# A graph layer on one core: the turn from its first phase to its second, written as one list of steps

## The chip, the core and the metric

The kernel runs on one core of a Trainium2 chip. The core has five engines with a queue of instructions each: TensorE (PE; its weight loads are PEld), VectorE (DVE), ScalarE (ACT), GpSimd (POOL) and SyncE (SP, which only issues transfers here). Each runs its own queue in order and waits on semaphores that the others count up. Transfers run on 16 DMA engines. The metric is the device time of the program in microseconds (us), from runs without a profiler.

## What is computed

The input has 6250 nodes of 256 features and 100000 edges, sorted by their target node, with 16 kinds of edge. Cut to what matters:

```python
xn = layernorm(x)
msg = einsum('ni,rio->rno', xn, W)[rel_type, src] * norm            # 16 relations
gnn = segment_sum(msg, dst)
k = softmax(xn @ Wk, over all nodes);  context = k.T @ (xn @ Wv)    # per head
mix = ((xn @ Wq) @ context) * sigmoid(gelu(ln(xn) @ Wg1 + bg1) @ Wg2 + bg2) @ Wproj + bproj
x1 = x + gnn + mix
t = layernorm(x1)
out = x1 + t + sum over e of combine[:, e] * (gelu(t @ w1[e] + b1[e]) @ w2[e] + b2[e])   # 8 experts, the best 2 weigh
```

## The kernel before

The nodes are 49 tiles of 128 (the last has 106), and two tiles make a pair; there are 24 pairs and one tile more. All products on TensorE are float32 as two reduced parts, a high and a low one, so that a product is three passes; where a part is not split, TensorE takes a float32 product as two instructions.

**The first phase** goes over the 49 tiles. It makes the 16 relations' rows of each tile and stores them to a table in HBM (SP issues four pieces for each tile, line 523), stores the key and value rows of each tile (`kv_d`), and from tile 24 on it also sums the first three edge blocks of each row of eight, and folds the keys of the tiles 0 to 23 into a running context.

**The second phase** goes over the pairs. A pair has eight groups of edge blocks (three and two blocks by turns, 20 in all; group S = 8 i + s). For each group GpSimd gathers the rows from the table, one indirect transfer for each block (`gathers`, line 814), into a ring of four groups, so that the gathers of group S wait until the sums of group S - 4 are done; ScalarE scales the rows (`MSGS`), VectorE makes the 0/1 selection (`SELECT`), TensorE sums (`SUMS`), VectorE adds the sums to the nodes (`adds`). Beside the groups of pair i stand the mixer of pair i - 1 (`OUT`, `GATES`, `GATE`, `PROJ`, `STATS`, `MEAN`, `NORM`, `TURN`), and the eight experts of pair i - 2 (`LAYER1`, `LOW`, `LAYER2`, `ADD`); the table `SLOTS_OF_PAIR` gives this order for eight slots. `STATS` gives the variances, GpSimd makes roots of them between two gathers (`roots2`, lines 823 and 824), and only then can `MEAN`, `NORM`, `TURN` and the first `LAYER1` of the pair follow.

**Between the two** stands the turn that is changed. The keys of the 25 tiles that are not yet folded in have to be shifted by their maximum, raised with Exp and multiplied with the values: four tiles are held in SBUF (`held_shifts`, `held_exps`, `held_contexts`), 21 come back from `kv_d` in six parts of four and three rows by turns (SP line 569; `shifts` line 1536, `exps` line 992, `contexts` line 1977). Parts 0 and 1 land in `slot`, the space of the first phase's edge sums, the others in `later`. When the last row is in, a chain of five steps turns the context into the weights of the query (`finish_context`, `context_turn`, `context_values`, `head_contexts`, `query_context`, `query_high`, `query_low`); the first `OUT` needs them. The experts' weights come in four chunks of 1 MB through two buffers (`load_chunk`, line 560) and are split by ScalarE (line 843) and VectorE (line 1182). In this turn the pairs 0 and 1 use the gathered rows whole (`WHOLE = 2`): no high and low parts, TensorE takes two float32 instructions of 256 columns for a block in place of two of the reduced kind. For pair 0 the slots hold only groups and the context; for pair 1 they are those of `SLOTS_OF_SECOND`; from pair 2 on those of `SLOTS_OF_PAIR`. So the experts of pair 0 other than the first two stand beside the groups of pair 2.

The order of the work on an engine is thus written out by hand, by slots: each engine runs, slot by slot, what the table names for it, with the work of the turn ahead of or behind the slot.

## Time and profile before

| what | value |
|---|---|
| time, three runs | 1601.41, 1601.22, 1599.69 us; median 1601.22 |
| span of the profiled execution | 1685.8 us, 84.6 us over the median |
| TensorE busy in it | 1601.8 us, 95% |
| VectorE, GpSimd, ScalarE busy | 79%, 59%, 57% |
| first phase | to about 779.7 us |
| turn, with the pairs 0 to 2 | about 779.7 to 891.4 us |
| each pair after that | about 34.0 us |

The profiled execution is one run with the profiler on; its own time is given only by its span, and it is longer than the runs without. Times of single instructions and distances between them are read from it; the median of the runs is what a change is counted against.
### The profile page before, as it was taken

What the parts mean: (1) busy time and instruction counts of PE and PEld (TensorE: products, weight loads), DVE (VectorE), ACT (ScalarE), POOL (GpSimd) and SP (SyncE); (2) the same over time, 40 slices, a digit from 0 to 9 for tenths busy, and PEclk for the clock granted to TensorE, in tenths of its full rate; (3) what the DMA queues carried; (4) which work ended last, traced back from release to release, by engine and by line L of the source; (5) the groups of instructions that cost most, each with busy time, mean ns of one, the idle gap of its engine ahead of it and who ended that gap; (6) DMA issues with size and microseconds to landing.
All of it is one profiled execution on the core that took longest, in us unless ns stands there. A gap on an engine that the chain in (4) does not pass through costs nothing.

```text
span 1685.8 us, 31748 instructions
## 1 busy us (share of the span) xinstructions
PE 1601.8 (95%) x10509; PEld 1451.7 (86%) x10509; DVE 1340.2 (79%) x3389; ACT 961.4 (57%) x2156; POOL 999.6 (59%) x1111
## 2 busy tenths in 40 slices
PE   7999999999999989998789999999999999999998
PEld 6888888777877878786689999999999999999998
DVE  7888565577777777775569999889999999999985
ACT  4444322345555555554566767667766777666764
POOL 4533322766676666673766767666766666666630
PEclk9999999999999999998999999999999999999999
DMA  9776656677877877787633333333333333333320
GB/s 295 267 258 246 235 226 238 222 242 242 259 249 242 257 228 252 238 265 271 203 98 100 108 104 112 100 102 101 117 101 106 101 116 100 99 109 110 104 62 10
DMA packets 127076, 290.50 MB, mean 172 GB/s; under 512 B 21271, under 2 KB 49724, under 8 KB 126914
## 3 DMA queue, kind: packets, MB, share of 16 engines
q1 hardware_dynamic: 86068, 177.19, 28.9%
q0 software_dynamic: 39952, 110.13, 24.1%
...
## 4 chain that ended last, share of the span: by engine, by line
PE 67%; DVE 12%; issue 8%; ACT 6%; another core or an unknown queue 3%; POOL 2%; DMA 1%; SPq 0%; DVEq 0%; ACTq 0%; POOLq 0%
PE bank L1821 52%; PE bank L2025 3%; PE bank L2026 2%; PE bank L1865 2%; PE bank L1866 2%; ACT mh L1030 2%; DVE ml L1606 2%; DVE ml_a L1357 1%; POOL stg L814 1%; PE bank L1977 1%; DVE ht L1722 1%; DVE xres L1736 1%; ACT raw L1086 1%; DVE stg L1224 1%
## 5 line engine op out<-in xcount | busy, mean ns | idle before, releaser
L814 POOL DMA_INDIRECT stg<-table,idxcur x495 | 530.6, 1072 | 263.9 <-issue 172.9
L1821 PE MATMUL bank<-wreg,xt 128*128 128x512 f32 x2352 | 589.9, 401 | 7.3 <-issue 6.5
L1821 PEld LDWEIGHTS bank<-wreg,xt 128*128 128x128 f32 x2352 | 438.6, 191 | 100.5 <-issue 11.4
L696 POOL DMA_INDIRECT raw<-table,idxa x297 | 302.5, 1018 | 147.3 <-issue 85.4
L1821 PE MATMUL bank<-tt,wreg 128*128 128x256 f32 (+1 forms) x2400 | 319.5, 282 | 0.0
L1821 PE MATMUL bank<-wreg,ht 128*128 128x256 f32 x2352 | 314.7, 283 | 0.4 <-DVE ht L1722 0.2
L1821 PEld LDWEIGHTS bank<-tt,wreg 128*128 128x128 f32 x2400 | 296.4, 189 | 2.9
L1821 PEld LDWEIGHTS bank<-wreg,ht 128*128 128x128 f32 x2352 | 293.2, 189 | 0.9 <-DVE ht L1722 0.4
L1086 ACT ACTIVATE raw<-bank,cols 128x256 f32<-128x256 f32 (+1 forms) x400 | 164.4, 462 | 132.7 <-remote 72.6
L1224 DVE COPY stg<-bank 128x512 f32<-128x512 f32 x196 | 134.2, 686 | 110.4 <-PE bank L1821 76.1
L1606 DVE SCALAR_TENSOR_TENSOR ml<-stg,nrm,mh 128x256 fp32r<-128x256 f32 x455 | 195.5, 478 | 13.4 <-ACT mh L1030 12.8
L860 ACT COPY stg<-bank 128x512 f32<-128x512 f32 x196 | 112.8, 582 | 156.3 <-PE bank L1821 124.8
L1030 ACT ACTIVATE mh<-stg,nrm 128x256 fp32r<-128x256 f32 x455 | 200.9, 499 | 0.0
L1736 DVE SCALAR_TENSOR_TENSOR xres<-bank,raw,xres 128x256 f32<-128x256 f32 x392 | 169.8, 473 | 21.6 <-PE bank L1821 11.7
L885 ACT ACTIVATE mh_a<-raw,nrm 128x256 fp32r<-128x256 f32 x297 | 128.9, 502 | 73.6 <-DMA raw<-table,idxa 49.6
L1091 ACT CAST ht<-raw 128x512 fp32r<-128x512 f32 (+1 forms) x200 | 122.5, 613 | 59.6 <-PE bank L1821 49.3
L1357 DVE SCALAR_TENSOR_TENSOR ml_a<-raw,nrm,mh_a 128x256 fp32r<-128x256 f32 x297 | 126.0, 477 | 37.1 <-issue 28.2
L1722 DVE TENSOR_TENSOR ht<-raw,ht 128x512 fp32r<-128x512 f32 (+1 forms) x200 | 134.9, 675 | 22.7 <-ACT ht L1091 20.6
L2025 PE MATMUL bank<-mh,sel 128*128 128x256 f32 x455 | 126.5, 304 | 4.1 <-DVE ml L1606 3.0
L2026 PE MATMUL bank<-ml,sel 128*128 128x256 f32 x455 | 118.4, 281 | 0.0
L1590 DVE TENSOR_TENSOR sel<-dbl,dpr 128x384 fp32r<-128x384 f32 x198 | 95.0, 480 | 9.8 <-PE bank L2021 7.7
L1865 PE MATMUL bank<-mh_a,sel_a 128*128 128x256 f32 x297 | 86.0, 314 | 13.3 <-DVE ml_a L1357 7.8
...
## 6 DMA issues: line engine op xcount, KB each, us to landing
...
```

The lines of the kernel that those rows point to most:

```text
L696: pool.indirect_dma_start(ring_a[:, r * EARLY + j, :], None, table[0:LIMIT, :], bass.IndirectOffsetOnAxis(ap=idxa[:, at:at + 1], axis=0)). ...
L814: pool.indirect_dma_start(stg[:, (s % 4) * SUP + j, :], None, table, bass.IndirectOffsetOnAxis(ap=idxcur[:, at:at + 1], axis=0)).then_inc( ...
L1030: act.activation(mh[:, (s % 2) * CUT + j, :], stg[:, (s % 4) * SUP + j, :], ACT.Copy, scale=nrm[:, bass.ds(at + j, 1)]).then_inc(msg_hi, 1)
L1086: act.activation(hf[e % 2][:, c * 256:c * 256 + nt * P], bank[2 + e % 2][:, c * 256:c * 256 + nt * P], ACT.Gelu, bias=b1c[:, 2 * e + c:2 * ...
L1224: dve.tensor_copy(stage[:, j // 2, (j % 2) * 512:(j % 2 + 1) * 512], bank[3 + j % 4][:]).then_inc(copied(k, j)[0], 1)
L1357: dve.scalar_tensor_tensor(out=ml_a[:, m + j, :], in0=ring_a[:, r * EARLY + j, :], scalar=nrm[:, bass.ds(EB * q + j, 1)], in1=halves(mh_a[ ...
L1606: dve.scalar_tensor_tensor(out=ml[:, m, :], in0=stg[:, (s % 4) * SUP + j, :], scalar=nrm[:, bass.ds(at + j, 1)], in1=halves(mh[:, m, :]), ...
L1722: dve.tensor_tensor(ht[e % 2][:, LO, :, 0:n], cols2(hf[e % 2], n), halves(ht[e % 2][:, HI, :, 0:n]), ALU.subtract).then_inc(h_lo, 1)
L1736: dve.scalar_tensor_tensor(out=xk, in0=bank[6 + e % 2][:, a * C:(a + 1) * C], scalar=comb[:, a, e:e + 1], in1=xk, op0=ALU.mult, op1=ALU.ad ...
L1821: mm = pe.matmul(dst, stat(a, c), mov(b, c), start=(n == 0), stop=(n == 3 * chunks - 1))
L2025: pe.matmul(bank[u % 2][:, 0:C], sel[:, m, :], mh[:, m, :], start=(s % 2 == 0 and j == 0), stop=False)
L2026: mm = pe.matmul(bank[u % 2][:, 0:C], sel[:, m, :], ml[:, m, :], start=False, stop=(s % 2 == 1 and j == PART[1] - 1))
```

## The change

- The slots of the pairs 0, 1 and 2 go. One list, `CHANGE`, holds all steps of the turn and of these pairs, and every engine runs in the list's order those steps that it has a part in (`follow`). From pair 3 on `SLOTS_OF_PAIR` is used as before.
- Five of the seven rows of `slot` are asked back by SP within the last tile of the first phase, behind its second table piece (`FREE_ROWS`); the other two follow the last of the kept contexts. VectorE's shifts and ScalarE's Exp of the parts 0 and 1 stand ahead of the wait for the end of the first phase.
- A weight chunk is split in two halves on each engine (`SPLIT n h`), and the splits stand elsewhere in the order.
- The first `LAYER1` of pair 0 stands ahead of the sums of group 11 (before: behind those of group 12), and experts of pair 0 stand among the last sums of pair 1. For this the experts' scratch (`hf`, `comb` and others) leaves the buffer of the weight chunks for space of its own (`cd`, `mix`, `wv`).
- Four groups more, 20 in all, use whole rows (`WHOLE_GROUPS`).
- The roots of pair 0 stand ahead of the second gather of group 12 (before: ahead of the first of group 13). The Gelu table is loaded early by a step of its own.

```diff
-    ROOTS, FIRST_ROOTS = (7, 1), (5, 0)
+    ROOTS, EARLIER_ROOTS = (7, 1), {1: (4, 1), 2: (5, 0)}
+    FREE_ROWS = 5
-        hf = [rs[:, 2048 + 512 * b:2560 + 512 * b] for b in range(2)]
+        ctxbd = cd[:, 0:C].rearrange("p (c n) -> p c n", c=CC)
+        dg = cd[:, C:2 * C]
+        hf = [cd[:], wv[:].rearrange("p c n -> p (c n)")]
...
@@ SP, stores of a tile @@
+                    if at(k, NT - 1) and h == 1:
+                        sp.wait_ge(sum_a, ER)
+                        for b2 in range(2):
+                            sp.wait_ge(kv_st[b2], 16 * ((KEPT + SLOTS) // 2))
+                        for n in range(FREE_ROWS):
+                            load_row(n // 4, n)
...
+            def load_row(part, n):
+                sp.dma_start(rows_of(part)[:, n, :], kv_d[group(group_of(part))[n]]).then_inc(kv_in[part], 16)
...
-            load_rows(0)
-            load_rows(1)
+            sp.wait_ge(ctx1_mm, KEPT)
+            for n in range(FREE_ROWS, SLOTS):
+                load_row(1, n)
             first_phase_over(sp)
...
             for n in range(4, 6):
-                sp.wait_ge(w_lo, n + 1)
+                sp.wait_ge(w_lo, splits_of(n, 1))
                 load_chunk(n + 2)
@@ ACT @@
+            def SPLIT(n, h):
+                act.wait_ge(raw_in[n % 2], 32 * (n // 2 - 1))
+                if n >= 6:
                     act.wait_ge(ctx_mm, HELD + REST)
+                act.copy(wreg[:, HI, place_of(n), h * CC // 2].rearrange("p r o -> p (r o)"),
+                         raw[:, n % 2, h * WC * C:(h + 1) * WC * C]).then_inc(w_hi, 1)
+            def GELU_TABLE():
+                act.activation(small[0:1, 156:157], small[0:1, 157:158], ACT.Gelu).then_inc(table_kept, 1)
             held_exps()
+            for ready in range(2):
+                EXP(ready)
             first_phase_over(act)
@@ DVE @@
+            for ready in range(2):
+                SHIFT(ready)
             dve.wait_ge(flag_ready, 1)
...
-PARTS_OF_SLOT = {0: (0, 1), 1: (2,), 2: (3,), 3: (4,), 4: (5,)}
-SPLITS = ((0, 4), (0, 5), (1, 0), (1, 1))
-SPLITS_LOW = ((0, 5), (0, 6), (1, 1), (1, 3))
-WHOLE = 2
+WHOLE_GROUPS = 20
...
+CHANGE = (
+    "HELD_ROWS", "ROWS_OF 0", "FADE", "SELECT 0 0", "SELECT 0 1", "SHIFT 2", "EXP 2", "ROWS_OF 1", "MSGS 0 0", "SUMS 0 0",
+    "ROWS_OF 2", "SHIFT 3", "EXP 3", "MSGS 0 1", "SUMS 0 1", "SELECT 0 2", "ROWS_OF 3", "SHIFT 4", "EXP 4",
+    "MSGS 0 2", "SUMS 0 2", "SHIFT 5", "EXP 5", "ADDS 0 0", "SELECT 0 3", "MSGS 0 3", "SUMS 0 3", "ROWS_OF 4",
+    "SELECT 0 4", "ADDS 0 1", "GELU_TABLE", "MSGS 0 4", "SPLIT 4 0", "SPLIT 4 1", "SELECT 0 5", "ROWS_OF 5",
+    "CONTEXT", "SUMS 0 4", "CONTEXT_PE", "MSGS 0 5", "CONTEXT_TURN", "SUMS 0 5", "VALUES", "SELECT 0 6", "HEADS",
+    "QUERY", "MSGS 0 6", "CLEAR", "ADDS 0 2", "QUERY_ROWS", "GATES 0 2", "GATE_ACT 0 2", "SUMS 0 6", "OUT 0 2",
+    "SELECT 0 7", "MSGS 0 7", "SPLIT 5 0", "SUMS 0 7", "SELECT 1 0", "GATE 0 2", "GATE_HI 0 2", "MSGS 1 0", "SUMS 1 0",
+    "ADDS 0 3", "GATE_LOW 0 2", "PROJ 0 2", "SELECT 1 1", "SPLIT 5 1", "MSGS 1 1", "SUMS 1 1", "ADDS 1 0", "STATS 0 2",
+    "SELECT 1 2", "MSGS 1 2", "SUMS 1 2", "SPLIT 6 0", "MEAN 0 2", "NORM 0 2", "SPLIT 6 1", "TURN 0 2", "TURN_HI 0 2",
+    "TURN_LOW 0 2", "MSGS 1 3", "SELECT 1 3", "LAYER1 0 2 0", "LOGIT 0 2", "SUMS 1 3", "LAYER1 0 2 1", "TOP 0 2",
+    "LOW 0 2 0", "ADDS 1 1",
+    "WEIGHT 0 2", "SELECT 1 4", "LOW 0 2 1", "SPLIT 7 0", "COMB 0 2", "COMB_HI 0 2", "MSGS 1 4", "LAYER1 0 2 2",
+    "LAYER2 0 2 0", "OUT 1 2", "SUMS 1 4", "GATES 1 2",
...
+    "ADD 0 2 6", "LAYER1 1 2 0", "LOGIT 1 2", "MSGS 2 5", "LAYER2 0 2 7", "LOW 1 2 0", "SUMS 2 5", "LAYER1 1 2 1", "TOP 1 2",
+    "ADD 0 2 7", "ADDS 2 2", "SELECT 2 6", "MSGS 2 6", "SUMS 2 6", "SELECT 2 7", "MSGS 2 7", "SUMS 2 7",
 )
...
+def follow(order, **steps):
+    for entry in order:
+        name, *numbers = entry.split()
+        if name in steps:
+            steps[name](*map(int, numbers), *((8,) if name in OF_GROUPS else ()))
...
-    for s in range(8):
-        slot_of(0, s, 8, None, 0, None, 0)
-    for s in range(8):
-        slot_of(1, s, 8, 0, 2, None, 0)
-    for i in range(2, pairs):
+    for i in range(3, pairs):
```

In the part of the list that is left out, the other steps of the experts of pair 0 (`LAYER1`, `LOW`, `LAYER2`, `ADD`) stand one by one among the groups 13 to 21, with the mixer of pair 1; `SPLIT 7 1` stands behind the sums of group 13.

## Rows read from the trace of the kernel before

**Rows 1.** Windows by stage: length, busy time and instructions by engine, clock, DMA share.

```profile
779.70:812.90 33.20, 28.75 (x122) 24.48 (x121) 13.34 (x22) 15.40 (x26) 21.73 (x25) 0.90 0.99 336
812.90:842.60 29.70, 19.44 (x98) 15.05 (x98) 19.91 (x38) 16.58 (x30) 22.69 (x20) 0.90 0.54 163
842.60:857.50 14.90, 10.62 (x50) 9.35 (x48) 4.71 (x16) 7.82 (x18) 9.43 (x11) 0.73 0.31 86
857.50:891.40 33.90, 33.36 (x278) 32.69 (x277) 28.73 (x77) 22.21 (x52) 22.92 (x26) 1.00 0.34 100
891.40:925.40 34.00, 33.18 (x278) 32.65 (x277) 31.09 (x88) 23.20 (x55) 23.83 (x24) 1.00 0.33 102
```

**Rows 2.** The chain of waits: start, us, what (tile, line, count).

```profile
798.61 3.47 PE bank L1977 x16
802.07 1.29 PE bank L2021 x6
...
891.46 4.20 PE bank L1821 x36
...
925.50 4.20 PE bank L1821 x36
```

**Rows 3.** Timeline of TensorE in the turn: start, us, instruction, [idle before <- releaser].

```profile
779.73 3.63 PE L1968 MATMUL bank<-kvs 128*128 128x257 f32 x16
787.80 8.64 PE L1977 MATMUL bank<-slot 128*128 128x257 f32 x28 [4.45 <-ACT slot L992]
...
806.67 6.23 PE L1977 MATMUL bank<-later 128*128 128x257 f32 x28
...
842.63 2.26 PE L1821 MATMUL bank<-tt,wreg 128*128 128x256 f32 x12
```

**Rows 4.** Timeline of SyncE's transfers, from the last tile on: start and us of issuing.

```profile
769.29 6.10 SPq L523 DMA_DIRECT2D table<-stg  x3
...
778.16 0.32 SPq L523 DMA_DIRECT2D table<-stg  x1
778.59 3.80 SPq L569 DMA_DIRECT2D slot<-kv_d  x7
782.84 7.04 SPq L569 DMA_DIRECT2D later<-kv_d  x14
```

**Rows 5.** Windows of 5 us, columns as in the first group.

```profile
770.00:775.00 5.00, 5.00 (x27) 4.19 (x26) 2.81 (x6) 2.92 (x6) 0.00 (x0) 1.00 0.53 211
...
785.00:790.00 5.00, 2.20 (x5) 1.83 (x6) 3.63 (x7) 1.91 (x2) 4.08 (x4) 0.57 1.02 348
```

**Rows 6.** Timeline of VectorE in the turn.

```profile
781.02 0.42 DVE L1379 TENSOR_TENSOR raw<-raw,bank 128x257 f32<-128x257 f32 x1 [0.47 <-DVE raw L1379]
785.43 1.23 DVE L1536 TENSOR_TENSOR slot<-slot,dg 128x1024 f32<-128x1024 f32 x1 [3.99 <-DMA slot<-kv_d]
...
817.64 2.27 DVE L1182 TENSOR_TENSOR wreg<-raw,wreg 128x2048 fp32r<-128x2048 f32 x1
...
833.59 0.25 DVE L1661 BATCH_NORM_AGGREGATE small<-small 128x2 f32<-128x6 f32 x2
...
839.80 0.68 DVE L1672 TENSOR_TENSOR tt<-bank,tt 128x512 fp32r<-128x512 f32 x1
```

**Rows 7.** Timeline of ScalarE: Exp of part 0, and the first gathered rows.

```profile
786.69 1.06 ACT L992 ACTIVATE slot<-slot 128x1024 f32<-128x1024 f32 x1 [6.09 <-DVE slot L1536]
...
791.50 1.31 ACT L1026 ACTIVATE stg<-stg,nrm 128x256 f32<-128x256 f32 x3 [2.21 <-DMA stg<-table,idxcur]
```

**Rows 8.** Timeline of GpSimd: gathers 1, 11, 21 and 43 of the second phase.

```profile
782.28 0.99 POOL L814 DMA_INDIRECT stg<-table,idxcur  x1 [1.27 <-DMA table<-stg]
...
798.53 0.94 POOL L814 DMA_INDIRECT stg<-table,idxcur  x1 [3.01 <-issue]
...
814.97 0.94 POOL L814 DMA_INDIRECT stg<-table,idxcur  x1 [3.85 <-issue]
...
849.05 0.95 POOL L814 DMA_INDIRECT stg<-table,idxcur  x1 [0.30 <-issue]
```

More of the change, by code:

```diff
@@ L804, in gathers @@
                     for j in range(PART[s % 2]):
-                        if (s, j) == (FIRST_ROOTS if isinstance(i, int) and i == 1 else ROOTS) and not (isinstance(i, int) and i < 1):
+                        if (s, j) == EARLIER_ROOTS.get(i, ROOTS) and not (isinstance(i, int) and i < 1):
                             roots2(i - 1, 2)
@@ L1022, in MSGS @@
                 at = EB * (4 * i + s // 2) + EARLY + (s % 2) * CUT
-                if isinstance(i, int) and i < WHOLE:
+                if whole(S):
                     for j in range(n):
@@ L1527, in _, with SHIFT @@
             keep_contexts(NT - 1, NP, 1, 0)
-            dve.wait_ge(flag_ready, 1)
-            far = dve.value_load(flag[0:1, 0:1], min_val=0, max_val=NT * P * R)
-            first_phase_over(dve)
-            def shifts(part):
+            def SHIFT(part):
                 a, b = span_of(part)
@@ L1766, in slot_of @@
             def slot_of(i, s, groups, p1, n1, p2, n2):
-                if isinstance(i, int) and i + s == 0:
-                    for part in PARTS_OF_SLOT[0]:
-                        shifts(part)
-                    fade_kept()
                 in_slot(i, s, groups, p1, n1, p2, n2, SELECT=SELECT, MSGS=MSGS, WINDOW=WINDOW, LAST_WINDOW=LAST_WINDOW, GATE=GATE,
@@ L1773, in slot_of @@
                         BIAS2_ADD=BIAS2_ADD, LOW=LOW, ADD=ADD)
-                if isinstance(i, int):
-                    if i == 0 and s > 0:
-                        for part in PARTS_OF_SLOT.get(s, ()):
-                            shifts(part)
-                    if (i, s) in SPLITS_LOW:
-                        split_lo(4 + SPLITS_LOW.index((i, s)))
-                if isinstance(i, int) and (i, s) == (0, 5):
-                    finish_context()
-                if isinstance(i, int) and (i, s) == (0, 6):
-                    head_contexts()
-                    dve.memset(halves(c3[:]), 0.0).then_inc(c3_clear, 1)
-                if isinstance(i, int) and (i, s) == (0, 7):
-                    query_low()
+            follow(CHANGE, SHIFT=SHIFT, FADE=FADE, SPLIT=SPLIT_LOW, CONTEXT=CONTEXT, CONTEXT_TURN=CONTEXT_TURN, HEADS=HEADS,
+                   CLEAR=CLEAR, QUERY_ROWS=QUERY_ROWS, SELECT=SELECT, MSGS=MSGS, ADDS=ADDS, GATE=GATE, GATE_LOW=GATE_LOW,
+                   STATS=STATS, MEAN=MEAN, TURN_LOW=TURN_LOW, TOP=TOP, COMB=COMB, COMB_LOW=COMB_LOW,
+                   BIAS2_ADD=BIAS2_ADD, LOW=LOW, ADD=ADD)
             run(slot_of, NP, TAIL_GROUPS)
@@ L1953, in _ @@
             pe.wait_ge(k_shift_diag, 2)
-            pe.matmul(bank[1][:, C:2 * C], halves(ones[:]), dg[:], start=True, stop=True).then_inc(kmb_mm, 1)
+            pe.matmul(bank[1][:, C:2 * C], halves(ones[:]), dg, start=True, stop=True).then_inc(kmb_mm, 1)
             pe.wait_ge(flag_ready, 1)
@@ L2151, in _ @@
             pe.wait_ge(add_a, ALL_ADDS)
+            follow(CHANGE, HELD_ROWS=HELD_ROWS, ROWS_OF=ROWS_OF, CONTEXT_PE=CONTEXT_PE, VALUES=VALUES, QUERY=QUERY,
+                   SUMS=SUMS, OUT=OUT, GATES=GATES, PROJ=PROJ, TURN=TURN, LOGIT=LOGIT, COMBT=COMBT, BIAS2=BIAS2,
+                   LAYER1=LAYER1, LAYER2=LAYER2)
             run(slot_of, NP, TAIL_GROUPS)
@@ L2181 @@
 )
[L2184 to L2193 removed]
+OF_GROUPS = ("SELECT", "MSGS", "SUMS", "ADDS")
+CHANGE = (
[4 rows of a table added]
+    "CONTEXT", "SUMS 0 4", "CONTEXT_PE", "MSGS 0 5", "CONTEXT_TURN", "SUMS 0 5", "VALUES", "SELECT 0 6", "HEADS",
[22 rows of a table added]
+)
+def follow(order, **steps):
[3 more added lines that the diff above has]
+            steps[name](*map(int, numbers), *((8,) if name in OF_GROUPS else ()))
 def in_slot(i, s, groups, p1, n1, p2, n2, **steps):
[L2199 removed]
+    for entry in SLOTS_OF_PAIR[s]:
         name, *expert = entry[1:].split()
```

156 lines of the change are left out of this document (62 added, 94 removed), and 12 rows, old and new, of the table CHANGE.

## The prediction, made before the changed kernel had run

> **What bounds the kernel now.** I read the stages first, then the chain of waits across the turn, then the timeline of each engine in it. The profiled execution spans 1685.8 us, 84.6 us more than the median of the runs (1601.2 us). I work out microseconds in the profiled execution and take the same number off the median; I have no row that says where the profiler's 84.6 us lie.
>
> From pair 3 on a pair takes 34.0 us, and TensorE is busy for 33.2 us of it at full clock [rows 1, 2]: the second phase is TensorE's. So the change can only move the instant at which this even pace begins: in the chain it begins with the 36 matmuls at 891.46 (`LAYER1 2` and `LAYER2 0` of pair 1, `OUT` of pair 2), and the next pair at 925.50 [rows 2]. I call 891.46 the hand-over. All work ahead of it is the same before and after, apart from four groups that become whole.
>
> The turn starts with the held rows at 779.73 [rows 3]; 111.7 us to the hand-over. In the first two stages TensorE is busy 28.75 of 33.2 and 19.44 of 29.7 us, in the third 10.62 of 14.9 at a mean clock of 0.73 [rows 1]. So some 19 us are idle, and part of the rest runs at half clock. The whole gain that is to be had lies there.
>
> **Part 1, key rows earlier.** Before, SP issues seven rows behind the last table piece, at 778.59 to 782.39 [rows 4]. VectorE is free at 781.44 and then waits 3.99 us for part 0; TensorE stands idle 4.45 us, and its next 28 matmuls take 8.64 us [rows 3, 6]. At full pace 16 such take 3.47 us [rows 2], so 28 take 6.07: 2.6 us went to the clock, whose mean is 0.57 in that window [rows 5]. After, five rows are issued behind table piece 1, that is between the first and the last of the three pieces issued from 769.29 to 775.39 [rows 4], by my reading at about 772 to 775. The DMA engines are 0.53 busy there [rows 5], so these rows should be in by 780. `SHIFT 0` can then start at 781.4, is 1.23 us, Exp 1.06 us [rows 6, 7], so TensorE goes on at about 783.8, against the held rows' end at 783.4. Idle and slow clock save 4.0 + 2.6 = 6.6 us at this place.
>
> Some is given back. The list puts `SUMS 0 0` ahead of part 2, and the scaling of the first gathered rows waits for their transfers until 791.50 + 1.31 [rows 7]. The first gather's own start, 782.28, waits for the last table piece (778.16) [rows 4, 8], and this isn't moved. So TensorE, through with part 1 at about 790, waits until about 792.3 for `SUMS 0 0`. What remains from there: the groups 0 to 3, 10 blocks of 0.43 (three take 1.29 [rows 2]) = 4.3, and 14 rows of 0.434 (two chunks of two instructions, 3.47 / 16 each, is 0.87 a row) = 12.1 us: 808.7. Before, the last row ended at 806.67 + 6.23 = 812.9 [rows 3]. **Term 1: -4.2 us.** Bounds: 0 (the DMA engines, 0.99 busy through this stage [rows 1], bring the later rows no sooner) and -6.6.
>
> **Part 2, from the last row to the first expert.** Before, the variances of pair 0 end at 833.84 (833.59 + 0.25), 20.9 us behind the last row. On that path VectorE's step on the heads stood behind a whole weight split of 2.27 us (817.64) [rows 6]. In the list `SPLIT 4` stands ahead of `CONTEXT`, while VectorE waits for the rows, and `SPLIT 5 0` behind `OUT`: 2.2 us go. **Term 2: -2.2.** Bounds 0 (another wait of VectorE, for `MSGS` or sums, in its place) and -4.9: gathers 21 on begin when `SUMS 0 4` is through, 814.97 now [rows 8]; by the list at 810.1, if the rows end at 808.7 and the three blocks follow.
>
> Then the first `LAYER1`. Before, 833.84 to 842.63 is 8.8 us [rows 3, 6]: `TURN_LOW` ended at 840.48, then three blocks of sums went first, 2.15 us. In the list these stand behind. GpSimd now waits for the variances with its roots (before it was busy with a gather, about 1.6 us), but one half of `SPLIT 6` comes between, about 1.2 us on VectorE and nearly as much on ScalarE; I let these cancel. **Term 3: -2.2**, bounds 0 and -3.8. The first `LAYER1` then starts at 842.6 - 8.6 = 834.0. The roots wait behind `STATS`: gather 32 and all behind it stand still until then, some 3 us by my times, counted with the gathers below.
>
> **Part 3, from the first expert to the hand-over.** Price list [rows 2]: a reduced matmul of 256 columns is 4.20 / 36 = 0.117 us; an expert's layer is 12 of them, 1.40. TensorE still has after `LAYER1 0`'s start: 18 layers (10 `LAYER1`, 8 `LAYER2`) 25.2; `OUT` and `PROJ` 2.8; the groups 11 to 19 whole, 22 blocks of 0.43, 9.5; groups 20 to 23, 10 blocks of two matmuls, 2.3; gates, turns, logits twice and biases, some 28 small ones (in a pair's 278 instructions [rows 1] 22 are such), 3.3. Sum 43.1 us. Before, the same stretch had 7 whole and 20 reduced blocks, so 25.2 + 2.8 + 3.0 + 4.7 + 3.3 = 39.0, and took 891.46 - 842.63 = 48.8 [rows 2, 3]: 9.8 us lost, nearly all ahead of 857.5.
>
> The four groups that become whole cost TensorE 10 x 0.2 = 2.0 us (in the 43.1) and save VectorE work that isn't on the path: it has 4.71 + 28.73 us in that stretch [rows 1], less than 37 even with two chunks' splits on top. After, there is expert work for TensorE wherever it waited for sums. I take the loss of an even pair (34.0 less 32.5 of work = 1.5; here 2.0) and one stretch of slow clock as after the idle of part 1 (2.6): 4.6 us. 834.0 + 43.1 + 4.6 = 881.7. **Term 4: 47.7 for 48.8, -1.1 us.** Bounds: a loss of 2.0 (-3.7) and of 9.8 (+4.1).
>
> At no cost: the merged buffers; SP's five issues (table pieces 2 and 3 become ready at about 775 and 778, behind them); the table load, which ends ahead of `MSGS 0 4` while the rows are on their way (uncovered it is one ACT step of about the size of an Exp); chunk 7, asked for when `SPLIT 5 1` is subtracted (about 823) and first needed behind 838.
>
> **Sum.** -4.2 - 2.2 - 2.2 - 1.1 = -9.7: hand-over at 881.7, span 1676, median 1601.2 - 9.7 = **1591.5 us**.
>
> **Rivals.**
>
> *The gathers set the pace.* 43 gathers took 782.28 to 850.0 [rows 8]; less the two stalls (3.01, 3.85) 1.42 us each, copies and roots in it. The first 60 then take 85 us, to 867.3; sums follow some 6 us later: 873, 8 us ahead of TensorE. But if both stalls stay (6.9) and the roots add 3, it is 883, and with one stall more 886: the gain is then 5 to 8 us, **1595**. For it: each of the 13 groups still needs its gathers. Against: the list lets TensorE clear the ring sooner.
>
> *The earlier rows bring nothing.* The stage is 0.99 full of transfers [rows 1], and if the table's last pieces, and with them the first gathers, get later for the five rows (5 x 128 x 513 x 4 bytes = 1.31 MB, 3.9 us at this stage's 336 GB/s), term 1 is lost and most of term 2, which leaves 2 to 4 us, **1599**. For it: nothing but transfers bounds 784 to 792. Against: 0.53 before that [rows 5], and piece 3 is only issued at 778.16 [rows 4], some 3 us behind the last of the five rows. I give it 0.13. The Trainium skill, "DMA: Bandwidth & Descriptors", section "Queues, rings and completion order", says that on each DMA engine the descriptors of SP's queue are consumed in ring order. By that rule the five rows go ahead of the pieces 2 and 3 and this rival comes out; no row of this trace shows two such transfers in each other's way.
>
> *Slower: the clock stays down.* From 842.6 to 857.5 TensorE ran at 0.73 though it had work for most of the time [rows 1]. In the list it has to wait for the roots at about 826 to 833, and then meets sums whose gathers may not be in, two groups between experts towards the end. If half of the 43.1 us (21.5 at full pace) runs at 1.2 in place of 2.4 GHz, that costs 21.5 us in place of my 2.6, and the time is 1591.5 + 19 = 1610; the gain is gone from about 10 us of such work beyond mine, and I put the case at **1606**. Against: experts are 1.4 us each and wait for nothing that is gathered. The Trainium skill, "TensorE: Matmul & The Clock Gate", Part 1, says that the throttled clock is the default and activity releases it; the drop behind the idle 4.45 us agrees with it.
>
> **How the numbers follow.** My forecast, 4 to 15 us gained (1586 to 1597), 0.57; gathers 0.15; rows bring nothing 0.13; slower 0.12; more than 15 us, 0.03. Within 0.2% (3.2 us) a measurement of this kernel can't be told from no change; nearly all of the third case lies there. Faster 0.76, same 0.12, slower 0.12. The range leaves out the gain over 16 us, which the gathers hardly allow (873), and most of the slower case: 1585 to 1602.
>
> **What would show it.** Right: rows end near 809, first expert near 834, the pair-3 matmuls near 882, and pairs of 34.0 behind; shifts of part 0 without a wait on a transfer; the clock full from about 838. Wrong: `SUMS 0 0` later than 794 (term 1); GpSimd's gather 21 still near 815 (term 2); TensorE idle or at half clock among the experts (term 4); a second pace in which gathers come back to back up to the hand-over.

## The result: slower, and the profile after

The changed kernel takes 1621.6 us (median of 4 runs, 1619.9 to 1623.9) against 1601.3 us for the kernel before on the same chip: a ratio of 1.0122 (95% interval 1.0104 to 1.0140), 20.3 us slower. 1591.5 was forecast, with 1602 as the upper end.

The rows of before that stand above come from an execution of 1685.8 us. In a second one, of 1600.0 us, the turn itself was 6.3 us shorter (the held rows' start to the hand-over: 105.4 for 111.7). I compare with that one from here on. These are its windows by stage: held rows to last key row, on to the first `LAYER1`, on to the hand-over, one pair. The columns are those of [rows 1].

```profile
721.70:753.80 32.10, 28.15 (x122) 24.04 (x121) 13.00 (x22) 14.56 (x25) 21.31 (x25) 0.95 1.03 346
753.80:783.50 29.70, 19.43 (x99) 14.99 (x97) 20.36 (x38) 17.54 (x30) 22.65 (x20) 0.89 0.54 165
783.50:827.20 43.70, 40.28 (x325) 39.30 (x324) 33.42 (x94) 29.91 (x67) 32.95 (x34) 0.99 0.36 104
827.20:860.40 33.20, 33.20 (x278) 32.72 (x277) 31.35 (x88) 23.73 (x56) 24.56 (x26) 1.00 0.37 108
```

The same four stages of the changed kernel:

```profile
718.90:751.00 32.10, 28.30 (x122) 23.93 (x121) 13.27 (x20) 16.14 (x28) 22.59 (x26) 0.95 0.95 316
751.00:779.20 28.20, 17.19 (x89) 13.66 (x88) 16.09 (x35) 13.83 (x27) 17.58 (x19) 0.84 0.55 170
779.20:845.30 66.10, 51.55 (x333) 47.84 (x334) 35.28 (x97) 34.16 (x77) 31.55 (x37) 0.91 0.26 76
845.30:878.40 33.10, 33.10 (x269) 32.96 (x269) 28.76 (x75) 21.50 (x49) 23.22 (x25) 0.95 0.35 101
```

The first stage is as long as before, the second 1.5 us shorter, the pair behind the hand-over as long. The third, from the first `LAYER1` to the hand-over, is 22.4 us longer. TensorE is busy for 51.55 of its 66.1 us. The prediction put its work there at 43.1 us; so 14.55 us are idle, and 8.4 us are busy time beyond that work. Before, it was 40.28 of 43.7 us for 39.0 us of work: 3.4 idle, 1.3 beyond.

Most of the 8.4 us is the slow clock, not all. These are the windows of the changed kernel's third stage whose granted clock lies furthest below 1:

```profile
779.20:784.00 4.80, 4.80 (x21) 4.74 (x22) 0.47 (x3) 1.46 (x3) 2.97 (x4) 0.50 0.36 96
784.00:789.00 5.00, 5.00 (x29) 4.71 (x28) 2.13 (x10) 1.20 (x3) 2.14 (x3) 0.68 0.14 44
832.00:838.00 6.00, 5.94 (x38) 5.73 (x38) 2.06 (x6) 2.27 (x5) 4.41 (x6) 0.75 0.33 101
```

Busy time times what the clock lacks of 1 gives 2.4, 1.6 and 1.5 us; the rest of the stage adds 0.2. That is an estimate of 5.6 us for the clock. The other 2.8 us aren't explained; a part may be that a row ahead of a wait counts to the end of its last matmul: the twelve at 796.63, ahead of a wait, take 1.58 us, while 1.39 us behind the start of the twelve at 795.24 the next row begins. Before, the mean clock of the stage was 0.99, so at most 0.4 of the 1.3 us is clock.

TensorE's timeline of before in its second execution, from the held rows to the hand-over:

```profile
721.71 3.63 PE L1968 MATMUL bank<-kvs 128*128 128x257 f32 x16
...
747.53 6.23 PE L1977 MATMUL bank<-later 128*128 128x257 f32 x28
...
783.47 1.99 PE L1821 MATMUL bank<-tt,wreg 128*128 128x256 f32 x12
...
827.11 1.57 PE L1821 MATMUL bank<-tt,wreg 128*128 128x256 f32 x12
```

And in the changed kernel:

```profile
718.88 3.63 PE L1979 MATMUL bank<-kvs 128*128 128x257 f32 x16
722.35 3.63 PE L1988 MATMUL bank<-slot 128*128 128x257 f32 x16
726.32 2.87 PE L1988 MATMUL bank<-slot 128*128 128x257 f32 x12 [0.34 <-ACT slot L1004]
732.65 2.90 PE L2032 MATMUL bank<-stg,sel 128*128 128x256 f32 x6 [3.47 <-ACT stg L1040]
...
744.75 6.23 PE L1988 MATMUL bank<-later 128*128 128x257 f32 x28
...
779.17 2.93 PE L1832 MATMUL bank<-tt,wreg 128*128 128x256 f32 x12 [2.66 <-DVE tt L1691]
...
800.00 1.10 PE L2032 MATMUL bank<-stg,sel 128*128 128x256 f32 x4 [1.78 <-ACT stg L1040]
...
805.19 1.53 PE L2032 MATMUL bank<-stg,sel 128*128 128x256 f32 x6 [1.26 <-ACT stg L1040]
...
831.89 0.55 PE L2036 MATMUL bank<-mh,sel 128*128 128x256 f32 x1 [2.73 <-DVE ml L1622]
...
843.05 0.36 PE L2036 MATMUL bank<-mh,sel 128*128 128x256 f32 x1 [2.60 <-DVE ml L1622]
...
845.23 2.76 PE L1832 MATMUL bank<-tt,wreg 128*128 128x256 f32 x12
```

The last row is the hand-over. Behind the first `LAYER1` each group of sums waits for its messages. The brackets of this stage add up to its idle 14.5 us: 7.1 us for ScalarE's messages (1.78, 1.26, 1.27, 1.27, 1.26 and 0.30), 5.9 us for the low parts of the last groups (2.73, 0.29, 2.60, 0.32), 1.46 us for a selection. ScalarE's timeline in one of these blocks says why the messages are late:

```profile
802.54 0.84 ACT L1100 ACTIVATE cd<-bank,cols 128x256 f32<-128x256 f32 x2 [1.35 <-PE bank L1832]
804.01 0.62 ACT L1105 CAST ht<-cd 128x512 fp32r<-128x512 f32 x1 [0.63 <-PE bank L1832]
804.54 1.30 ACT L1040 ACTIVATE stg<-stg,nrm 128x256 f32<-128x256 f32 x3
```

The messages (line 1040) wait for no transfer: they stand in the list behind `LAYER1`'s copy, and the copy waits for TensorE's `LAYER2` of two experts earlier. TensorE then does `SUMS` and waits for the messages; the next expert waits behind the sums. GpSimd meanwhile waits for TensorE, not TensorE for it:

```profile
807.51 0.94 POOL L830 DMA_INDIRECT stg<-table,idxcur  x1 [2.99 <-PE bank L2032]
```

So in this block TensorE and ScalarE take turns: the first layers at 795.24, 800.75 and 806.70 are 5.5 and 6.0 us apart, where the even pace has eight slots in 33.2 us, 4.2 each.

### The profile page after: what moved, and what is told of

It reads as the page before. It is cut to its first block, busy times and chain, and to the rows that moved or that the text cites. A ratio compares the mean times of both kernels' runs of the same rounds, so it can differ in the third digit from the quotient of the medians.

```text
span 1618.1 us, 31745 instructions
## 1 busy us (share of the span) xinstructions
PE 1571.3 (97%) x10509; PEld 1441.1 (89%) x10509; DVE 1338.5 (83%) x3383; ACT 966.3 (60%) x2161; POOL 1010.4 (62%) x1111
## 3 DMA queue, kind: packets, MB, share of 16 engines
q8 instruction: 85, 1.39, 0.4%
## 4 chain that ended last, share of the span: by engine, by line
PE 90%; DVE 3%; issue 2%; ACT 2%; DMA 1%; POOL 1%; SPq 0%; ACTq 0%; DVEq 0%; POOLq 0%
PE bank L1832 71%; PE bank L2036 4%; PE bank L2037 3%; PE bank L1876 2%; PE bank L1877 2%; PE bank L2032 1%; PE bank L1887 1%; PE bank L1988 1%; PE bank L2076 1%; PE bank L2088 1%; DMA xres<-in_L_gnn_weight 1%; PE bank L1842 1%; DVE pad L1262 1%; PE bank L2085 1%; DMA stg<-table,idxcur 0%
## 5 line engine op out<-in xcount | busy, mean ns | idle before, releaser
L830 POOL DMA_INDIRECT stg<-table,idxcur x495 | 543.1, 1097 | 238.5 <-issue 149.1
L1832 PE MATMUL bank<-wreg,xt 128*128 128x512 f32 x2352 | 578.1, 396 | 0.9 <-DVE wreg L1189 0.4
L1832 PEld LDWEIGHTS bank<-wreg,xt 128*128 128x128 f32 x2352 | 432.9, 188 | 88.8 <-ACT stg L872 1.2
L1622 DVE SCALAR_TENSOR_TENSOR ml<-stg,nrm,mh 128x256 fp32r<-128x256 f32 x445 | 190.9, 477 | 15.3 <-ACT mh L1044 15.2
L1044 ACT ACTIVATE mh<-stg,nrm 128x256 fp32r<-128x256 f32 x445 | 196.4, 499 | 0.3 <-PE bank L2037 0.3
L1755 DVE SCALAR_TENSOR_TENSOR xres<-bank,mix,xres 128x256 f32<-128x256 f32 x392 | 169.4, 472 | 18.2 <-PE bank L1832 17.5
L1100 ACT ACTIVATE wv<-bank,cols 128x256 f32<-128x256 f32 (+1 forms) x200 | 82.5, 464 | 68.4 <-PE bank L1832 68.4
L1100 ACT ACTIVATE cd<-bank,cols 128x256 f32<-128x256 f32 (+1 forms) x200 | 82.5, 463 | 46.3 <-PE bank L1832 46.3
L677 POOL TENSOR_TENSOR xres<-xres,bpb 128x256 f32<-128x256 f32 x24 | 20.7, 863 | 131.4 <-DVE kvs L1224 131.3
L2036 PEld LDWEIGHTS bank<-mh,sel 128*128 128x128 f32 x445 | 84.2, 189 | 11.5 <-issue 6.2
```

The source lines that it names most:

```text
L830: pool.indirect_dma_start(stg[:, (s % 4) * SUP + j, :], None, table, bass.IndirectOffsetOnAxis(ap=idxcur[:, at:at + 1], axis=0)).then_inc( ...
L1044: act.activation(mh[:, (s % 2) * CUT + j, :], stg[:, (s % 4) * SUP + j, :], ACT.Copy, scale=nrm[:, bass.ds(at + j, 1)]).then_inc(msg_hi, 1)
L1100: act.activation(hf[e % 2][:, c * 256:c * 256 + nt * P], bank[2 + e % 2][:, c * 256:c * 256 + nt * P], ACT.Gelu, bias=b1c[:, 2 * e + c:2 * ...
L1622: dve.scalar_tensor_tensor(out=ml[:, m, :], in0=stg[:, (s % 4) * SUP + j, :], scalar=nrm[:, bass.ds(at + j, 1)], in1=halves(mh[:, m, :]), ...
L1755: dve.scalar_tensor_tensor(out=xk, in0=bank[6 + e % 2][:, a * C:(a + 1) * C], scalar=comb[:, a, e:e + 1], in1=xk, op0=ALU.mult, op1=ALU.ad ...
L1832: mm = pe.matmul(dst, stat(a, c), mov(b, c), start=(n == 0), stop=(n == 3 * chunks - 1))
```

## The experiments

For each kernel the table gives three instants, in us from the start of its held rows in its profiled execution (the first phase ends at 718.9 to 725.0, differently in each execution, so spans alone don't compare), the stretch from the first `LAYER1` to the hand-over, and the timed runs. The kernel before has 32.1, 61.8, 105.4 and 43.6; the changed one 32.1, 60.3, 126.4 and 66.1. The runs come from several chips, so times are compared by the ratios, each against the kernel before on the same chip.

| Kernel | rows end | first LAYER1 | hand-over | stretch | median us | ratio to before (95%) |
|---|---|---|---|---|---|---|
| e1, before again | 32.1 | 61.8 | 105.4 | 43.6 | 1601.7 (one run) | |
| e2, messages ahead | 32.9 | 61.1 | 119.5 | 58.4 | 1613.9 | 1.0063 (1.0043 to 1.0084) |
| e4, 16 whole groups | 32.5 | 60.6 | 129.5 | 68.9 | 1627.0 | 1.0146 (1.0122 to 1.0170) |
| e3b, rows late | 34.1 | 60.6 | 126.8 | 66.2 | 1622.9 | 1.0120 (1.0103 to 1.0137) |
| e5, e2 + split 6 late | 33.6 | 60.0 | 118.2 | 58.2 | 1613.0 | 1.0054 (1.0034 to 1.0074) |
| e6, e5 + rows 2 first | 32.7 | 61.0 | 117.3 | 56.3 | 1608.8 | 1.0034 (1.0021 to 1.0047) |
| e7, experts in the old pace | 32.1 | 60.3 | 113.0 | 52.7 | 1608.5 | 1.0033 (1.0021 to 1.0046) |
| e13, old second half | 32.9 | 62.0 | 107.7 | 45.7 | 1601.2 | 0.9999 (0.9988 to 1.0009) |
| e8, a list for each engine | 26.3 | 54.7 | 115.2 | 60.6 | 1611.2 | 1.0051 (1.0033 to 1.0069) |
| e9, e8 with rows late | 31.7 | 61.4 | 117.7 | 56.3 | 1612.2 | 1.0055 (1.0037 to 1.0072) |
| e10, two sums to an expert | 25.4 | 55.2 | 121.1 | 65.9 | 1616.0 | 1.0073 (1.0056 to 1.0090) |
| e11, e8 + old pace | 26.3 | 56.1 | 109.6 | 53.4 | 1602.6 | 0.9995 (0.9985 to 1.0005) |
| e12, e11 mended | 25.8 | 54.8 | 104.6 | 49.8 | 1599.1 | 0.9979 (0.9964 to 0.9995) |

**e1, the kernel before once more, for a second profile.** No edit. It gave the windows above.

> The kernel before, unchanged, once more with a profile, since its first profiled execution was 84.6 us longer than its runs while that of the changed kernel (1618.1 us) agrees with its runs. If the surplus lay in the first phase (TensorE idle there), the held rows start at about 719 us as in the changed kernel, and turn plus pairs behind it make up the difference of 20 us: hand-over about 107 to 112 us behind the held rows, against 126.4 in the changed kernel. If the change also costs time in the first phase, the held rows start some 5 us earlier than 719.

**e2, the messages ahead on ScalarE.** The list of the changed kernel, with `MSGS` of groups 1 4 to 2 6 moved ahead of the `LAYER1` beside them:

```diff
-    "ADDS 1 2", "LAYER1 0 2 4", "LAYER2 0 2 2", "MSGS 1 6",
+    "ADDS 1 2", "MSGS 1 6", "LAYER1 0 2 4", "LAYER2 0 2 2",
```

> Only the order is changed: in the blocks with experts of pair 0 the scaling of the gathered rows (MSGS of groups 12 to 22) goes ahead of the expert's first layer in the list, as in the slots used before. Theory A (ScalarE's order): behind the first layer, ScalarE's copy of the hidden rows waits for TensorE's second layer, the scaling waits behind the copy and TensorE's sums wait for the scaling, which costs 1.3 to 2.7 us in each block, 14.6 us in the eleven gaps of the trace: about 1605 to 1609 us. Rival B (the gathers are late): the scaling would wait for its transfers in the new place too, no gain, 1619 to 1622. Rival C (whole rows load TensorE): no gain here either.

The idle time of the stretch fell from 14.5 to 7.7 us (2.22, 0.72, 2.31 and 2.47), the hand-over came 6.9 us sooner, the time fell by 8 to 9 us. TensorE's busy time hardly fell (50.67 us, at a mean clock of 0.88 for 0.91), so the slow clock didn't go with these waits. ScalarE's order is a third of the loss; it isn't all.

**e4, fewer whole groups.**

```diff
-WHOLE_GROUPS = 20
+WHOLE_GROUPS = 16
```

> The changed kernel with 16 whole groups in place of 20: groups 16 to 19 take a high and a low part. Rival C: 10 blocks cost TensorE 0.2 us less each, 2 us gained, 1619 to 1620. Theory A: VectorE's low parts come into the serial loop of each block as well, each group later by 0.9 to 1.3 us: 2 to 6 us slower, 1624 to 1628.

Not faster: the hand-over comes 3.1 us later, and the time is 3.8 us longer by the ratios, whose intervals overlap. So the larger load of TensorE isn't the cause of the loss. That the four whole groups help where sums stand among experts is likely, but not shown.

**e3b, the five early rows issued behind the last table piece again.**

```diff
-                    if at(k, NT - 1) and h == 1:
-                        sp.wait_ge(sum_a, ER)
...
-                        for n in range(FREE_ROWS):
-                            load_row(n // 4, n)
```

> The changed kernel with one thing undone: its first five key rows come back as late as in the kernel before, behind the last table piece. The list of steps stays. Theory A (the early rows brought nothing at the rows' end: in the changed kernel's trace the rows end 32.1 us after the held rows' start, as in the kernel before, 32.05): 1621.6 within 2.5 us, and the rows end at +32 to +34. Rival (the early rows are worth what was forecast): 3 to 5 us slower than the changed kernel, some 1626. Rival (the early rows delay the table's last pieces and the first gather, which starts at +4.07 for +2.64 before): 1 to 2 us faster, some 1620, with the first gather at +2.6.

The median is 1.3 us above the changed kernel's and the ratio the same; the rows end 2.0 us later, the first `LAYER1` comes 0.3 and the hand-over 0.5 us later. In this list the early rows bring nothing that lasts. Their price shows too. First SyncE and GpSimd of the changed kernel:

```profile
710.35 3.91 SPq L554 DMA_DIRECT2D slot<-kv_d  x5
714.36 0.38 SPq L539 DMA_DIRECT2D table<-stg  x1
715.59 0.32 SPq L551 DMA_DIRECT2D hg_d<-hgt  x1
...
721.01 0.31 POOL L757 MEMSET cd<- 128x256 f32 x1 [21.39 <-DMA hg_d<-hgt]
...
722.95 0.99 POOL L830 DMA_INDIRECT stg<-table,idxcur  x1 [0.29 <-POOL idxcur L752]
```

And of e3b:

```profile
719.29 0.32 SPq L545 DMA_DIRECT2D hg_d<-hgt  x1
...
721.22 0.31 POOL L756 MEMSET cd<- 128x256 f32 x1 [14.46 <-DMA hg_d<-hgt]
...
724.43 0.99 POOL L829 DMA_INDIRECT stg<-table,idxcur  x1 [1.37 <-DMA table<-stg]
```

GpSimd, which waits for `hg_d`, goes on 5.4 us after its issue behind five rows, and 1.9 us without them. The first gather starts 4.1 us behind the held rows' start for 2.7. The Trainium skill, "DMA: Bandwidth & Descriptors", section "Queues, rings and completion order", has the descriptors of SyncE's queue consumed in ring order; the 5.4 for 1.9 us agree with it. But the 16 DMA engines were busy for 0.98 of those 5.4 us (715.59 to 721.01) and for 0.25 of the 1.9 us (719.29 to 721.22), so engines full of rows account for the delay as well; no run separates the two.

**e5 and e6, the halves of split 6, and the third part of the rows.** Each on top of the one before:

```diff
-    "SUMS 1 2", "SPLIT 6 0", "MEAN 0 2", "NORM 0 2", "SPLIT 6 1", "TURN 0 2",
+    "SUMS 1 2", "MEAN 0 2", "NORM 0 2", "TURN 0 2",
...
-    "TURN_LOW 0 2", "MSGS 1 3", "SELECT 1 3", "LAYER1 0 2 0",
+    "TURN_LOW 0 2", "MSGS 1 3", "SELECT 1 3", "SPLIT 6 0", "SPLIT 6 1", "LAYER1 0 2 0",
...
-    "ROWS_OF 1", "MSGS 0 0", "SUMS 0 0", "ROWS_OF 2",
+    "ROWS_OF 1", "MSGS 0 0", "ROWS_OF 2", "SUMS 0 0",
```

> As e2 (messages ahead of the first layer's copy on ScalarE, 1613.9), and both halves of the split of weight chunk 6 moved from before and behind the normalisation to just ahead of the first expert's first layer. Theory A (the halves lie on the path from the roots to the first LAYER1, 2.2 us of it, and the engine's clock is down behind that wait): the first LAYER1 starts at +58 to +59 for +61.1 in e2, and the time is 1610 to 1612. Rival (the roots on GpSimd and the rest of the chain end last anyway): within 1.5 us of e2, the first LAYER1 at +60.5 or later.

> As e5, and the third part of the key rows goes ahead of the first sums in TensorE's order (the changed kernel let TensorE wait 3.47 us for the first message there, while the third part's exponential had been done 2.3 us before). Theory A (that order cost the rows' end): the rows end at +29 to +30 for +32 to +33, and the time is 2 to 3 us below e5. Rival (the rows' end is set by the landing of the later parts, or what follows waits for something else): the rows end within 1 us of e5's, and the time is within 1.5 us of e5's.

The first `LAYER1` comes 1.1 us sooner with e5, and that is lost again in e6's run. The times differ by 0.9 and 4.2 us, the hand-overs by 1.3 and 0.9 only, with overlapping intervals. With e5 the way from the variances to the first `LAYER1` takes 5.7 us for 7.4, so the halves did lie on the path, as its theory had it; but the time stayed within 1.5 us of e2, as the rival had it. The rows end with e6 within 1 us of e5, as its rival had it: putting part 2 first exchanged the wait for messages for one of 2.20 us for part 2's Exp, at half clock (5.42 us for 16 matmuls). Whether e6 gains time isn't told: its time fell by more than the rival's 1.5 us, its hand-over by 0.9.

**e7, the experts in the old pace.** Up to `TURN_LOW` the changed list with its roots, then `LAYER1 0 2 0`, the sums of groups 1 3 to 1 7 with `LAYER1 0 2 1` among them, and from `WEIGHT` on `SLOTS_OF_PAIR` written out for pair 2's groups, one to a slot (pair 2's groups in two products, as in the kernel before):

```diff
+    "MSGS 1 3", "SELECT 1 3", "LAYER1 0 2 0", "LOGIT 0 2", "SUMS 1 3",
...
+    "SUMS 1 5", "SELECT 1 6", "MSGS 1 6", "ADDS 1 2", "LAYER1 0 2 1", "SUMS 1 6", "SPLIT 7 0", "SPLIT 7 1",
+    "SELECT 1 7", "MSGS 1 7", "SUMS 1 7", "WEIGHT 0 2", "SELECT 2 0", "LOW 0 2 1", "MSGS 2 0",
...
```

> The changed kernel's list up to the first LAYER1 of pair 0, then the old order: the rest of pair 1's sums in a row beside the first two first layers, and the experts 2 to 7 with pair 2's groups in the even pace's own order. Theory A (the loss is in the list from the first LAYER1 on: 66.1 us for 43.1 us of work): that stretch takes 44 to 48 us as in the kernel before (43.8), and the time is 1600 to 1605. Rival B (gathers late, since GpSimd's first gather starts 1.4 us later and the roots are issued earlier): the stretch stays above 55 us, and the time above 1611. Rival C (the two-product sums moved to whole groups, or the split chunks, load the engine): the stretch stays above 55 us with TensorE's busy share above 0.95.

13.4 us of the hand-over are regained, not 21. Idle is 4.4 us here, but TensorE is busy for 48.31 of 52.7 us at a mean clock of 0.86: the first `LAYER1` still takes 2.93 us. It lies between the theory and its rivals: part of the loss must come from what e7 kept, the first `LAYER1` ahead of the sums and the early roots, or from the first half. It also has 16 whole groups again, as have e11, e12 and e13.

**e13, the new first half with the old second half.** As e7, but sums 1 3 and 1 4 ahead of the first `LAYER1`, and the roots at their old place:

```diff
+    "SELECT 1 3", "MSGS 1 3", "SPLIT 6 0", "MEAN 0 2", "NORM 0 2", "SPLIT 6 1", "SUMS 1 3", "SELECT 1 4", "ADDS 1 1",
+    "TURN 0 2", "TURN_HI 0 2", "MSGS 1 4", "TURN_LOW 0 2", "SUMS 1 4", "SELECT 1 5", "LAYER1 0 2 0", "LOGIT 0 2",
...
-    ROOTS, EARLIER_ROOTS = (7, 1), {1: (4, 1), 2: (5, 0)}
+    ROOTS, EARLIER_ROOTS = (7, 1), {1: (5, 0)}
```

> The changed kernel's list as far as the sums of group 1 2 (its early key rows, its order of rows and chain, its halves of the splits), and behind that the old kernel's order: sums of groups 1 3 and 1 4 ahead of the first LAYER1, the other three between it and the second, experts 2 to 7 in the old pace with pair 2's groups in two products, the roots at the old places. Theory (the whole loss comes from moving pair 1's sums behind the first LAYER1 and among the experts, and the first half is worth about nothing): pair 3's pace at +104 to +109 for +105.4 in the kernel before and +126.4 in the changed one, and 1600 to 1605 us. Rival (the first half also costs, by the later first gather and the split halves on the path): pace at +111 or later, 1607 or more. Other rival (the first half gains what was forecast, 8.6 us, once the second half does not hide it): pace at +101 or sooner, 1597 or less.

It takes as long as the kernel before. So the early rows, the order of rows and chain and the halved splits are together worth nothing that can be measured, and the whole loss lies in what the change does from group 1 3 on (experts, roots, whole groups). TensorE's timeline of e13 around the first `LAYER1`:

```profile
773.42 4.61 PE L2032 MATMUL bank<-stg,sel 128*128 128x256 f32 x10 [3.54 <-issue]
777.82 1.06 PE L2076 MATMUL bank<-ident,scr 128*128 128x128 f32 x4
780.05 1.53 PE L2032 MATMUL bank<-stg,sel 128*128 128x256 f32 x6 [1.17 <-DVE xres L1636]
781.24 1.75 PE L1832 MATMUL bank<-tt,wreg 128*128 128x256 f32 x12
```

The ten matmuls of groups 1 2 and 1 3 run at half clock (4.61 us; at full clock ten take 2.32) while the normalisation is worked out on other engines. The 3.54 us of idle time ahead of them stand in the changed kernel too: the sums of 1 2 start 0.6 us behind their selection in both kernels (773.42 behind 772.79, and 772.31 behind 771.68), which stands behind `STATS` on VectorE. The first `LAYER1` comes 1.7 us later than in the changed kernel, but takes 1.75 us for 2.93. In the changed kernel 1 3 is behind it. There the clock is already down when `TURN` comes (its four matmuls at 775.39 take 1.12 us for 0.60), TensorE then stands still for 2.66 us, and the experts pay for the slow clock: in the windows from 779.20 on, shown with the result, TensorE is busy throughout, at a granted clock of 0.50 (1.2 for 2.4 GHz) and then 0.68.

**e8 and e9, a list for each engine.** `CHANGE` becomes a list per engine; all rows go first, the sums into the waits of the chain. On VectorE:

```diff
-    "SELECT 0 0", "SELECT 0 1", "SHIFT 2", "SHIFT 3", "SELECT 0 2", "SHIFT 4", "SHIFT 5", "ADDS 0 0",
+    "SELECT 0 0", "SELECT 0 1", "SHIFT 2", "SHIFT 3", "SHIFT 4", "SHIFT 5", "SELECT 0 2", "ADDS 0 0",
```

> The steps of the changed kernel in a list of its own for each engine: all key rows ahead of the sums on VectorE, ScalarE and TensorE (the shifts of the last parts no longer behind a selection that waits for the first sums), the sums then in the waits of the chain from the context to the first LAYER1, halves of the weight splits in VectorE's waits, only six of pair 1's and pair 2's groups fewer behind the first LAYER1 than in the changed kernel, and messages ahead of the first layer's copy on ScalarE. Theory (each wait of the changed turn is one of order, and the gathers leave room): rows end at +26 to +28 for +32.1, first LAYER1 at +50 to +54 for +60.3, pair 3's pace at +95 to +102 for +126.4 (kernel before: +105.4), and 1590 to 1600 us. Rival (the gathers, which start at +4 to +6 with the early rows, set the pace through the sums that the chain needs): the first LAYER1 at +56 or later and 1603 or more.

> As e8, with the first five key rows as late as in the kernel before (behind the last table piece). Theory (the early rows hold up the landing of the last node's gate rows, which GpSimd waits for, and with it the first gather; with the sums in the chain's waits an earlier gather is worth more than earlier rows): first gather at +2.7 for +4 to +6, rows end at +28 to +30, first LAYER1 1 to 3 us sooner than in e8, and 1 to 3 us below e8. Rival (the rows set the chain's start and the gathers have room): 2 to 4 us above e8.

Here the rows do end sooner, at 26.3, and the first `LAYER1` comes at 54.7. What held the rows is to be seen on VectorE, first in e6, then in e8:

```profile
742.82 0.56 DVE L1605 TENSOR_TENSOR sel<-dbl,dpr 128x384 fp32r<-128x384 f32 x1 [4.61 <-PE bank L2032]
743.30 2.09 DVE L1545 TENSOR_TENSOR later<-later,cd 128x1024 f32<-128x1024 f32 x2
```

```profile
738.33 1.23 DVE L1545 TENSOR_TENSOR later<-later,cd 128x1024 f32<-128x1024 f32 x1 [2.80 <-DMA later<-kv_d]
741.49 0.96 DVE L1545 TENSOR_TENSOR later<-later,cd 128x768 f32<-128x768 f32 x1 [1.94 <-DMA later<-kv_d]
```

In e6 `SELECT 0 2` (the first row) waits 4.61 us for sums, and the shifts of parts 4 and 5 behind it then wait for no transfer: their rows were there. In e8 the shifts wait for the rows alone. With that gone the early rows are worth 5.4 us at the rows' end and 6.7 at the first `LAYER1` (e9 against e8), but 1.0 us of the time. The theory of e9, that the early rows cost more through the later gather than they bring, fell at these instants; the times can't tell the two apart. And all of the gain of e8 is gone at the hand-over: the stretch takes 60.6 us, and pace and time are far off what I expected.

**e10, e11 and e12, what stands behind the first LAYER1.** All from e8's first half; e10 has two groups to an expert, e11 has groups 1 4 to 1 6 ahead of the old pace and 1 7 in its first slot, e12 mends four places of e11, one of them on GpSimd:

```diff
-    ROOTS, EARLIER_ROOTS = (7, 1), {1: (4, 0)}
+    ROOTS, EARLIER_ROOTS = (7, 1), {1: (4, 0), 2: (6, 1)}
```

> As e8 up to the first LAYER1 (which e8 had at +54.7, 5.6 us sooner than the changed kernel), and behind it the same steps in another order: the experts' layers start at once, the sums that are left come two to an expert up to expert 6, so that pair 2's first two groups, which pair 1's statistics wait for, are summed by expert 5 and not by experts 5 and 6 with the turn behind the last expert. Theory (in e8 and in the changed kernel the pair's last chain, from the statistics through roots, normalisation and turn to the next pair's first LAYER1, lies bare behind expert 7, since its sums come too late: 816 to 836 in e8): no wait over 1 us there, pair 3's pace at +100 to +107 for +115.2 in e8, and 1595 to 1603 us. Rival (VectorE and ScalarE can't do two groups to an expert beside the layers): blocks of 6 to 7 us, pace at +112 or later, and 1608 or more.

> As e8 up to the first LAYER1, then pair 1's last groups ahead of the experts 2 to 7, and these in the old kernel's even pace with pair 2's groups one to a slot (the roots of pair 1 at the old place, all pair 2 groups in two products). Theory (the lists of rows and chain are worth some 7 us against the old kernel, and the experts in the old pace give none of it back): pair 3's pace at +100 to +104, 1595 to 1600 us, faster than the old kernel (1602.8) by 3 to 7. Rival (the gathers of pair 1's last groups, landing at +61 to +68, then set the start of the pace): pace starts at +72 or later, and 1602 to 1608.

> As e11, with four places mended that its trace names: pair 1's roots on GpSimd go ahead of five gathers (e11 had the statistics at 811.9 and the roots at 815.8, behind the gathers), the first LAYER1 goes ahead of the sums of group 1 3 on TensorE (e11's waited 1.3 us for these messages), the messages of group 1 4 ahead of the second first layer's copy on ScalarE (2.1 us), and the combination weights ahead of the third first layer's copy. Theory (the pair's chain behind the statistics costs the pace in e11 40.5 us for 32.9 in the kernel before): pace starts at +66 to +67 for +69.0, pair 3's pace at +100 to +104 for +109.6 in e11 and +105.4 in the kernel before, and 1594 to 1599 us. Rival (VectorE's and ScalarE's load in the pace with both halves of the last split and two-product sums, not the roots, made it slow): pair 3's pace at +107 or later, 1600 to 1603.

e10 is the slowest of the three: its theory fell. GpSimd waits 6.72 us with pair 1's roots, the gathers behind them come late, and the messages of group 2 4 wait 4.37 us for their transfer:

```profile
812.64 0.23 POOL L839 TENSOR_SCALAR small<-small 128x2 f32<-128x2 f32 x1 [6.72 <-DVE small L1680]
```

```profile
819.45 1.30 ACT L1044 ACTIVATE mh<-stg,nrm 128x256 fp32r<-128x256 f32 x3 [4.37 <-DMA stg<-table,idxcur]
```

e11 gives the opposite: it has the statistics at 811.62 and the roots only at 815.84, behind gathers, and `TURN` waits for it:

```profile
815.84 0.24 POOL L839 TENSOR_SCALAR small<-small 128x2 f32<-128x2 f32 x1
```

```profile
818.35 0.66 PE L2076 MATMUL bank<-ident,scr 128*128 128x128 f32 x4 [2.86 <-ACT scr L1065]
```

In e12 the roots start 0.2 us behind the statistics (813.43 for 812.96 + 0.25), that wait is 0.78 us, and the first slot to the hand-over takes 36.8 us for 40.5. e12 is 0.2% faster than the kernel before (0.9979, 0.9964 to 0.9995): the one version that beats both, at the edge of what can be told. The theory's 1594 to 1599 was reached only at its upper end, and its hand-over of 100 to 104 us was missed by little (104.6), since the pace still takes 36.8 us for 32.9 and the first `LAYER1` is still at half clock (2.93 us).

## Why the prediction was wrong

The instants against the kernel before in its 1600.0 us execution:

| Term | forecast | measured | from |
|---|---|---|---|
| 1, the rows' end | -4.2 | 0.0 | 32.1 for 32.1 |
| 2, to the variances | -2.2 | -0.1 | 20.8 for 20.9 |
| 3, to the first LAYER1 | -2.2 | -1.4 | 7.4 for 8.8 |
| 4, to the hand-over | -1.1 | +22.4 | 66.1 for 43.6 |
| sum | -9.7 | +20.9 | time: +20.3 |

**Term 4 is the step that failed, and it alone gives the sign.** I counted TensorE's work (43.1 us, which I still take) and set its loss at 4.6 us, since "there is expert work for TensorE wherever it waited for sums". The list doesn't allow that: each engine works in its order, so an expert behind `SUMS` waits when the sums wait. I priced TensorE's row of the list and never followed ScalarE's, where each message stands behind a copy that waits for TensorE. The loss was 23.0 us: 14.5 idle, some 5.6 by the slow clock, 2.8 open. The runs share out the 21.0 us at the hand-over so: 13.4 go when the experts stand in the old pace (e7), and of these ScalarE's order alone is worth 6.9 (e2); 5.3 more go when sums 1 3 and 1 4 stand ahead of the first `LAYER1` and the roots at their old place (e13, both together). The last 2.3 don't show in the time, which is that of the kernel before. What low parts, selections and clock are each worth stands only in rows, and no run separates them.

**The rivals.** The one on the other side named the right place, "meets sums whose gathers may not be in", and the clock, at 0.12 and 1606; of its two parts the clock was some 5.6 us and the waits were the larger, but not for gathers: the messages were in (the row at 804.54 waits for no transfer). The gathers did not set the pace; GpSimd waits for TensorE in this stretch. And 1621.6 lies beyond even its 1606. That the earlier rows bring nothing came out (e3b); that the late landing of `hg_d` is a part of it is likely, not shown.

**Term 1.** Part 0 was shifted without a wait, as forecast (719.46). But two rows of part 1 are still issued at 719.07, and its shift waited 3.75 us; then TensorE waited 3.47 us for the first message, with the gather 1.4 us later than before, and ran at half clock (2.90 us for six). I had that message at 12.6 us behind the held rows' start; its sums began at 13.8. That `SELECT 0 2` stands ahead of the shifts of parts 4 and 5 I didn't see; in e8, where it stands behind them (among other moves), the rows end at 26.3.

**Term 2.** The whole split is off the chain, yet the variances are as late: VectorE waits 2.62 us for the sums of groups 1 0 and 1 1, which the statistics need, the bound that I had named. The variances of before (second execution) and VectorE in the changed kernel:

```profile
774.43 0.25 DVE L1661 BATCH_NORM_AGGREGATE small<-small 128x2 f32<-128x6 f32 x2
```

```profile
768.81 0.88 DVE L1636 TENSOR_TENSOR xres<-bank,xres 64x256 f32<-64x256 f32 x2 [2.62 <-PE bank L2032]
771.52 0.25 DVE L1680 BATCH_NORM_AGGREGATE small<-small 128x2 f32<-128x6 f32 x2
```

These sums are late for the reason of term 4: their messages wait for no transfer, but stand on ScalarE behind `GATE_HI`, which waits for VectorE's `GATE`:

```profile
762.17 0.62 ACT L1058 CAST xtp<-scr 128x512 fp32r<-128x512 f32 x1 [2.36 <-DVE scr L1660]
762.69 1.30 ACT L1040 ACTIVATE stg<-stg,nrm 128x256 f32<-128x256 f32 x3
```

**Term 3.** Its gain was mostly there; with the halves of split 6 off the path (e5) the way takes 5.7 us for 7.4. But it was no gain: the sums that it moved back had kept TensorE at work while the chain waited.

The profile that I worked from was an execution with a loss of 9.8 us in that stretch; e1 has 4.7. So more was there to gain in the rows that I read than in a usual run, which didn't change the sign.
